# Softmax shift of both heads of a pair by VectorE, and rough maxima folded in SBUF, in a latent-attention and mixture-of-experts kernel

## The reference, cut to what matters

```python
x = x + layernorm(attention(layernorm(x)))      # x: (1, 2048, 256), float32
x = x + layernorm(moe(layernorm(x)))            # 16 experts of width 128, top 2, one shared expert

def attention(x):                               # 16 heads, latent keys and values of rank 64
    q = (x @ wq)                                # 128 + 64 columns a head, the 64 rotated
    ckv, k_pe = split(x @ wkv_a)                # 64 + 64, rms-normalised, rotated
    k_nope, v = split(ckv @ wkv_b)
    scores = einsum(q, k) * 192 ** -0.5         # causal mask
    attn = softmax(scores)
    return einsum(attn, v) @ wo
```

## Time and profile before

| | us |
|---|---|
| median of 3 runs | 1501.66 |
| lowest and highest of them | 1495.69, 1503.52 |
| span of the profiled execution, first to last instruction | 1484.4 |
| median of the runs less that span | 17.3 |
| TensorE matmul busy | 1299.4 (88%) |
| VectorE busy | 935.3 (63%) |
| GpSimd busy | 851.6 (57%) |
| ScalarE busy | 644.3 (43%) |

### The profile page before, as it was taken

How to read it: one execution, slowest core, us unless ns; L and a number is a source line. 1 busy time by engine, 2 the same in 40 slices (tenths; PEclk the granted TensorE clock), 3 DMA queues, 4 the chain that set the end, 5 groups by cost and what they waited for, 6 DMA issues and landing times.

```text
span 1484.4 us, 26542 instructions
## 1 busy us (share of the span) xinstructions
PE 1299.4 (88%) x7260; PEld 634.1 (43%) x7261; DVE 935.3 (63%) x2026; ACT 644.3 (43%) x1321; POOL 851.6 (57%) x900
## 2 busy tenths in 40 slices
PE   3989988899999789999999979999999999868830
PEld 2544564344446423333334632333333333647620
DVE  5555557654534777777663687767777683565536
ACT  3553535244443514444444432444444445347632
POOL 0073426566662747777777364778777778225535
PEclk9999999799999969999999977999999999979975
DMA  8000000000000000000000000000000000046754
GB/s 276 1 1 0 0 15 29 1 0 0 0 0 15 29 1 1 0 0 0 0 0 15 29 22 11 22 21 11 11 21 21 21 11 11 15 112 189 194 143 131
DMA packets 42931, 51.26 MB, mean 35 GB/s; under 512 B 5824, under 2 KB 39744, under 8 KB 42432
## 3 DMA queue, kind: packets, MB, share of 16 engines
q1 hardware_dynamic: 36816, 37.37, 8.1%
q0 software_dynamic: 4864, 10.51, 3.2%
...
## 4 chain that ended last, share of the span: by engine, by line
PE 69%; DVE 13%; issue 6%; POOL 5%; DMA 3%; ACT 3%; DVEq 0%; POOLq 0%; SPq 0%; ACTq 0%
PE ps L1386 17%; PE ps L1202 10%; PE ps L1333 9%; PE ps L1203 9%; PE ps L1204 9%; PE ps L1362 5%; DVE mxp L834 4%; PE ps L1478 2%; DMA B<-xn_rows,tok_i 2%; POOL C L404 1%; DMA B<-in_L_attn_x 1%; POOL A L411 1%; PE ps L1462 1%; POOL C L408 1%; PE ps L1364 1%
## 5 line engine op out<-in xcount | busy, mean ns | idle before, releaser
L395 POOL TENSOR_TENSOR D<-D,B 128x512 f32<-128x512 f32 (+3 forms) x512 | 551.6, 1094 | 118.4 <-ACT B L525 112.7
L525 ACT ACTIVATE B<-ps 128x512 f32<-128x512 f32 (+3 forms) x640 | 335.0, 533 | 530.5 <-DVE ps L854 209.5
L834 DVE TENSOR_REDUCE mxp<-ps 128x1 f32<-128x512 f32 (+3 forms) x640 | 378.5, 605 | 190.6 <-PE ps L1333 130.0
L1386 PE MATMUL ps<-B,kv 128*64 128x512 f32 (+3 forms) x1280 | 290.1, 549 | 0.0
L1333 PE MATMUL ps<-KTh,A 128*128 128x512 f16 (+3 forms) x640 | 233.5, 378 | 27.9 <-DVE mxp L834 18.5
L1202 PE MATMUL ps<-A,KTh 128*128 (+3 forms) x640 | 225.8, 353 | 2.7 <-issue 2.3
L1203 PE MATMUL ps<-A,KTh 128*128 (+3 forms) x640 | 224.6, 351 | 0.0
L1204 PE MATMUL ps<-A,KTl 128*128 (+3 forms) x640 | 223.9, 350 | 0.0
L854 DVE TENSOR_TENSOR ps<-ps,D 128x512 f32<-128x512 f32 x224 | 143.2, 639 | 92.2 <-PE ps L1364 54.9
L388 POOL TENSOR_TENSOR D<-B 128x512 f32<-128x512 f32 (+1 forms) x64 | 76.3, 1199 | 195.8 <-ACT B L525 195.8
L1333 PEld LDWEIGHTS ps<-KTh,A 128*128 (+1 forms) x640 | 62.9, 99 | 227.7 <-issue 118.6
...
...
## 6 DMA issues: line engine op xcount, KB each, us to landing
...
```

Source lines behind the costliest of these rows:

```text
L395: nc.gpsimd.tensor_tensor(acc[:, c0:], acc[:, c0:], Pr[:, i % P_RING, c0:], ALU.add).then_inc(sum_done, 1)
L525: nc.scalar.activation(Pr[:, i % P_RING, c0:], ps[:, i % ST_RING, c0:], ACT.Exp, scale=SM_SCALE).then_inc(exp_done, 1)
L834: V.tensor_reduce(mxp[:, s, i4, kc:kc + 1], ps[:, 4 + j % MX_RING, 0:w], AX.X, ALU.max).then_inc(mx_free, 1)
L1386: T.matmul(ps[LORA * s:LORA * (s + 1), BK_O, c0:], kv[:, kt, 0:LORA], Pr[:, i % P_RING, c0:], start=(kt == 0), stop=(kt == KT - 1)).then_i ...
```

## The change

The fourth matmul and `Dm` go, in all chunks. VectorE shifts both heads of a pair in all chunks, in one add over the two banks of a key tile (`shift`), and ScalarE takes exp over two banks in one instruction, GpSimd adds both heads in one. The scores ring is two pairs of banks (`ST_RING = 2`), the ring of probabilities four pairs (`P_RING = 4`); both hold as many key tiles as before.

The rough scores come in batches of two matmuls into the two banks 4 and 5 (`BK_X`; for a chunk's first pair also 0, 1 and 2, 3). ScalarE copies a batch to SBUF as bf16 (`take_rough`). VectorE folds there with `max` (`refine`): step by step the chunks of 512 keys into the first, then the half into the half down to 64 columns, then one reduction to `mrow`. TensorE spreads the maxima with four matmuls of `mrow` broadcast by a negated identity (`spread`), and ScalarE copies them out (`widen`). `early`, `refine_at` and `spread_at` say at which key tile of the pair each of these stands. The values of the last two key tiles of a pair move behind the first scores of the next pair, and the copy of the output with them.

```diff
-        CR_EXP, CR_PV, CR_SUM, CR_MX, CR_L, CR_O, CR = ST_RING, P_RING, P_RING, MX_RING, 2, 1, 2
+        CR_EXP, CR_PV, CR_SUM, CR_MX, CR_M, CR_L, CR_O, CR = ST_RING, P_RING, P_RING, 1, 2, 2, 1, 2
+        def batch(qc, b):
+            s, r = b // (tiles_of(qc) // 2), b % (tiles_of(qc) // 2)
+            kc, i0 = r // 2, 2 * (r % 2)
+            return s, kc, i0, CQ if kc < qc else P * (i0 + 2)
...
+        def early(qc):
+            n, every = tiles_of(qc), {0: (1, 2), 1: (2, 3), 2: (3, 4), 3: (3, 4)}[qc]
...
+                take = min(n - b, 2 if kt % every[0] == 0 else 1)
...
+        def spread_at(qc):
+            n = tiles_of(qc)
+            return (n - 3, n - 1) if qc > 1 else (n - 2, n - 1)
...
-                            nc.gpsimd.tensor_tensor(acc[:, c0:], acc[:, c0:], Pr[:, i % P_RING, c0:],
+                        nc.gpsimd.tensor_tensor(acc[:, :, c0:], acc[:, :, c0:], Pr[:, kt % P_RING, :, c0:],
...
+            def take_rough(qc, p, b):
+                act.wait_ge(mx_ready, first_kt(qc) + p * tiles_of(qc) + b + 1)
...
+                copy(dst[:, i0:i0 + 2, 0:w], ps[:, bk:bk + 2, 0:w]).then_inc(mx_out, 1)
+            def widen(qc, p, s):
+                act.wait_ge(wide_ready, 2 * (qc * NP + p) + s + 1)
+                copy(minus_m[:, p % 2, s, :], ps[:, BK_M, :]).then_inc(wide_done, 1)
+                for kt in range(KT):
+                    if len(new):
+                        take_rough(qc, p + 1, new[0])
+                    act.wait_ge(shifted, n + 1)
+                    nc.scalar.activation(Pr[:, kt % P_RING, :, c0:], ps[:, 2 * (kt % ST_RING):2 * (kt % ST_RING) + 2, c0:],
+                                         ACT.Exp, scale=SM_SCALE).then_inc(exp_done, 1)
+                    if kt == LAG - 1 and behind:
+                        values_out(qc, p - 1)
+                    if len(new) > 1:
+                        take_rough(qc, p + 1, new[1])
+                    if ahead and kt in spread_at(qc):
+                        widen(qc, p + 1, spread_at(qc).index(kt))
...
+            def refine(qc, p, s, k):
+                base, ring = rough(qc)
+                acc, chunk = base[:, s], ring[:, (s * qc + k) % 2]
+                if k:
+                    dve.wait_ge(mx_step, done)
...
+                if k == folds(qc) - 1:
+                    V.tensor_reduce(mrow[:, s, :], acc[:, :, 0:P // 2], AX.X, ALU.max).then_inc(m_ready, 1)
+                elif k >= max(qc, 1):
+                    h = (P // 2) << (folds(qc) - 2 - k)
+                    V.tensor_tensor(acc[:, :, 0:h], acc[:, :, 0:h], acc[:, :, h:2 * h], ALU.max).then_inc(mx_step, 1)
...
+                elif k == qc - 1:
+                    for i in range(TC):
+                        w = P * (i + 1)
+                        V.tensor_tensor(acc[:, i, 0:w], acc[:, i, 0:w], chunk[:, i, 0:w], ALU.max
+                                        ).then_inc(mx_step, 1)
+                else:
+                    V.tensor_tensor(acc, acc, chunk, ALU.max).then_inc(mx_step, 1)
             def shift(qc, p, kt):
-                V.tensor_tensor(ps[:, i % ST_RING, c0:], ps[:, i % ST_RING, c0:], minus_m[:, p % 2, c0:],
+                V.tensor_tensor(ps[:, bk:bk + 2, c0:], ps[:, bk:bk + 2, c0:], minus_m[:, p % 2, :, c0:],
                                 ALU.add).then_inc(shifted, 1)
+                for kt in range(KT):
+                    shift(qc, p, kt)
                     if ahead:
+                        for s, k in refine_at(qc)[kt]:
+                            refine(qc, p + 1, s, k)
+                    if kt == KT // 4 and sums is not None:
                         part_sums(qc, sums)
...
-                        ins = T.matmul(dst, ones4, Dm[:, p % 2, s, c0:], start=False, stop=(j < 0))
+                def spread(p, s):
+                    pe.wait_ge(m_ready, CR_M + k + 1)
+                    for j in range(TC):
+                        ins = T.matmul(ps[:, BK_M, j * P:(j + 1) * P], mrow[:, s, j:j + 1].broadcast_to([P, P]),
+                                       negident, start=True, stop=True)
+                    for kt in range(KT):
+                        new = early(qc)[kt] if ahead else ()
+                        scores(p, kt)
+                        if len(new):
+                            rough_batch(p + 1, new[0])
+                        if kt >= LAG:
+                            values(p, kt - LAG)
+                        elif behind:
+                            values(p - 1, KT - LAG + kt)
+                        if len(new) > 1:
+                            rough_batch(p + 1, new[1])
+                        if ahead and kt in spread_at(qc):
+                            spread(p + 1, spread_at(qc).index(kt))
```

More of the change, by code:

```diff
@@ new lines, in folds, with step_incs, folds_before, step_base @@
+        def folds(qc):
+            return qc + 4 if qc else 3
+        def step_incs(qc, k):
+            if qc == 0:
+                return (3, 1, 0)[k]
+            return ((1,) * (qc - 1) + (TC, 1, 1, 1, 0))[k]
+        def folds_before(qc, s, k):
+            return s * sum(step_incs(qc, i) for i in range(folds(qc))) + sum(step_incs(qc, i) for i in range(k))
+        def step_base(qc, p):
+            return sum(NP * folds_before(q, 2, 0) for q in range(qc)) + p * folds_before(qc, 2, 0)
+        def step_needs(qc, s, k):
+            last = s * (qc + 1) + (min(k + 1, qc) if qc else 0)
+            return 2 * last + 2
@@ new lines, in early, with refine_at @@
+        def early(qc):
+            n, every = tiles_of(qc), {0: (1, 2), 1: (2, 3), 2: (3, 4), 3: (3, 4)}[qc]
+            out, b = [], 0
+            for kt in range(n):
+                take = min(n - b, 2 if kt % every[0] == 0 else 1)
+                out.append(range(b, b + take))
+                b += take
+            return out
+        def spread_at(qc):
+            n = tiles_of(qc)
+            return (n - 3, n - 1) if qc > 1 else (n - 2, n - 1)
+        def refine_at(qc):
+            n, out, todo = tiles_of(qc), [], [(s, k) for s in range(2) for k in range(folds(qc))]
+            done = 0
+            for kt in range(n):
+                now = []
+                while todo and step_needs(qc, *todo[0]) <= done and (len(now) < 2 or kt == n - 1):
+                    now.append(todo.pop(0))
+                out.append(now)
+                done += len(early(qc)[kt])
+            return out
@@ L1339, in turn_max, with rough_batch @@
[L1339 to L1349 removed]
+                KT = tiles_of(qc)
+                def rough_batch(p, b):
+                    s, kc, i0, _ = batch(qc, b)
+                    n = first_kt(qc) + p * KT + b
+                    bk = rough_bank(p, b)
+                    pe.wait_ge(mx_out, n + 1 if bk == BK_X and b == 0 or not isinstance(p, int) or p
+                               else first_kt(qc) + max(b - 2, 0) + 1)
+                    for i in range(2):
+                        w = CQ if kc < qc else P * (i0 + i + 1)
+                        wide = w if qc else P * (i0 + 2)
+                        ins = T.matmul(ps[:, bk + i, 0:wide], QTh[:, bass.ds((2 * p + s) * CQ + (i0 + i) * P, P)],
+                                       KTh[:, kc * CQ:kc * CQ + wide], start=True, stop=(kc < qc))
+                        if kc == qc:
+                            ins = T.matmul(ps[:, bk + i, w - P:w], identb, mask_qk, start=False, stop=True)
+                    ins.then_inc(mx_ready, 1)
@@ L1377, in values @@
+                    for s in range(2):
+                        bk = 2 * (kt % ST_RING) + s
+                        q = bass.ds((2 * p + s) * CQ + c0, CQ - c0)
+                        ins = three(ps[:, bk, c0:], KTh[:, keys], KTl[:, keys], QTh[:, q], QTl[:, q], True, j < 0)
+                        if j >= 0:
+                            ins = T.matmul(ps[:, bk, c0:c0 + P], identb, mask_kq, start=False, stop=True)
+                    ins.then_inc(st_ready, 1)
                 def values(p, kt):
@@ L1407, in pair @@
+                    ins.then_inc(pv_done, 1)
+                def pair(p, ahead=True, behind=True):
                     for kt in range(KT):
-                        score_unit(p, 2 * kt)
-                        between()
-                        score_unit(p, 2 * kt + 1)
-                        between()
+                        new = early(qc)[kt] if ahead else ()
+                        scores(p, kt)
+                        if len(new):
+                            rough_batch(p + 1, new[0])
@@ L1421, in _ @@
                     pe.wait_ge(where_ready, qc)
-                for j in range(U):
-                    max_unit(0, j)
-                    if j == U // 2 + 2:
-                        turn_max(0, 0)
-                turn_max(0, 1)
-                if qc >= SHIFT_FROM:
-                    for h in range(2):
-                        spread(0, h)
-                with pe.Fori(0, NP - 1) as p:
-                    pair(p, True)
-                pair(NP - 1, False)
+                for b in range(KT):
```

(11 more changed lines are left out.)

302 lines of the change are left out of this document (118 added, 184 removed).

## The result

| | before | after |
|---|---|---|
| median, us | 1501.55 (4 runs, 1495.69 to 1503.52) | 1655.53 (4 runs, 1649.91 to 1660.71) |
| ratio, with its 95% interval | | 1.1044 (1.1001 to 1.1087) |
| span of the profiled execution | 1484.4 | 1658.8 |

The kernel became 10% slower: the direction of the forecast, but 111 us beyond its 1544 and 50 beyond the range. The span grew by 174.4 us, the median by 154. The profile of before lies 17 us under its median, that of after 3 over its own. A run's time is about 2 us above its own span (1660.71 and 1658.8 in the profiled execution of after), so the profiled execution of before was itself some 15 us faster than the median.

The account below looks back on a forecast made before the run. TensorE was taken to bound the pairs before; after, VectorE's work, waits and idle time. Pairs +56, last pairs -9 and first rough maxima -5 gave +42: span 1526 us, median 1544 us, range 1420 to 1605.

Parts of the forecast that it names:

- Folds by bytes: VectorE's bf16 folds: priced at half the fp32 row's time per element, 0.08 us + 0.52 ns per element.
- Rival D: VectorE's folds cost the fp32 row's price per element and bound the pairs: +120 us, 1664 us; chance 0.05.
- VectorE's work: Shifts, folds, part sums and cuts per pair: 30.3, 21.5, 14.4 and 7.3 us in chunks 3 to 0.
- its waits: VectorE's folds and cuts waiting for GpSimd's adds, per pair: 14.7, 9.2, 7.5, 2.5 us in chunks 3 to 0.
- period per pair = work + waits + idle: VectorE's time as the pair's period: 50.0, 35.7, 25.6 and 11.3 us in chunks 3 to 0.
- the pairs' term: Longer periods of seven pairs in each chunk: 7 x 8.05 = +56 us.
- rival C: Halfway: waits of three quarters of those forecast leave the pairs unchanged, 1495 to 1509 us; chance 0.07.
- Rival B: VectorE's waits fit into slack, under half of 14.7 us in chunk 3's pairs: faster, 1437 us; chance 0.33.
- Rival E: TensorE's stops at pair ends bring the low clock for a fifth of each pair: 1610 us; chance 0.05.
- Last pairs: Each chunk's last pair has no folds and only loses its row matmuls: -9 us.
- First rough maxima: Maxima for each chunk's first pair: chunk 3 from 25.9 to about 20.5 us, -5 us in all.
- Costed at nothing: Constants, semaphore setting and the moved output copy lie beside the next pair's matmuls: nothing, otherwise at most 1 us a chunk.

Follow-up runs that it names:

- after_no_adds: The changed kernel with GpSimd's adds cut to one column per head, except the first of each pair; 1492.64 us, ratio 0.996 to the kernel before.
- after_no_folds: The changed kernel with each VectorE fold cut to one column, GpSimd's adds whole; 1534.43 us, ratio 1.0258 to the kernel before.
- after_half_adds: The changed kernel with each GpSimd add split in two, one of 512 columns per head; 1617.93 us, ratio 1.0817 to the kernel before.
- after_heads: The changed kernel with scores, shift and exp done head by head instead of over two banks; 1644.92 us, ratio 1.099 to the kernel before.
- before_no_adds: The kernel before with GpSimd's adds one column wide except the first of each head and pair; 1497.56 us, ratio 0.9993 to the kernel before.

## Why the prediction was wrong

**The mechanism was right.** It was taken from two cuts that folds and adds shut each other out. after_no_adds and after_no_folds show from either side that both are needed for the loss, after_half_adds that a single fold waits by the length of an add. The Trainium skill (SBUF — State Buffer, Who interferes with whom) has it as a rule, and these runs agree, with 1.22 us alone and up to 3.34 beside an add.

**The prices were right.** Folds by bytes: 1.22 us for 2048 (1.2 taken), 0.35 for 384 (0.28), and 1.02 for the four small ones (1.0). Rival D is out. The shift is 1.14 from start to start, adds are 2.36 us in the median and 3.23 at the longest (2.37 and 3.5).

**VectorE's work was right, its waits right or too high.** Its busy time per pair in after_no_adds, where nothing waits, is 30.2, 21.5, 14.6 and 7.3 us in chunks 3 to 0, against 30.3, 21.5, 14.4 and 7.3. In after its busy share of the windows times the period gives 44.1, 28.8, 19.4 and 7.7. The differences are the waits: 13.9, 7.3, 4.8 and 0.4 us against 14.7, 9.2, 7.5 and 2.5. Chunk 3 came out nearly as counted, the shorter chunks had fewer waits. By kind in chunk 3, the single folds wait 4.1 us (4.5 taken), the runs 8.1 (6.6), the short groups nothing (1.0), the cuts 2.2 (2.6).

**The step that failed is the idle time in "period per pair = work + waits + idle".** I gave VectorE 5.0, 5.0, 3.7 and 1.5 us, "in a pair's first three key tiles". What is left of the period is 10.5, 12.2, 8.6 and 4.7. Over one pair of each chunk that is 20.8 us of idle too few against 7.4 of work and waits too many; the net 13.4, times seven, is 94, and the pairs' term missed by 149 - 56 = 93. Most of this idle time lies where I had put it, and is longer. Here are the first four shifts of a pair of chunk 3, in after and then in after_no_adds:

```profile
1226.13 1.23 DVE L959 TENSOR_TENSOR ps<-ps,D 128x1024 f32<-128x1024 f32 x1 [3.26 <-PE ps L1288]
1229.58 1.23 DVE L959 TENSOR_TENSOR ps<-ps,D 128x1024 f32<-128x1024 f32 x1 [2.21 <-PE ps L1288]
1231.81 1.23 DVE L959 TENSOR_TENSOR ps<-ps,D 128x1024 f32<-128x1024 f32 x1 [0.99 <-PE ps L1288]
1235.12 1.23 DVE L959 TENSOR_TENSOR ps<-ps,D 128x1024 f32<-128x1024 f32 x1 [2.08 <-PE ps L1288]
```

```profile
1044.81 1.23 DVE L959 TENSOR_TENSOR ps<-ps,D 128x1024 f32<-128x1024 f32 x1 [2.09 <-PE ps L1288]
1048.26 1.23 DVE L959 TENSOR_TENSOR ps<-ps,D 128x1024 f32<-128x1024 f32 x1 [2.21 <-PE ps L1288]
1050.49 1.23 DVE L959 TENSOR_TENSOR ps<-ps,D 128x1024 f32<-128x1024 f32 x1 [1.00 <-PE ps L1288]
1053.80 1.23 DVE L959 TENSOR_TENSOR ps<-ps,D 128x1024 f32<-128x1024 f32 x1 [2.08 <-PE ps L1288]
```

In after VectorE stands idle 8.5 us before these four, and 1.8 later in the pair. Without adds it is 7.4 before the same four, and the distances are the same to 0.01 us (3.45, 2.23, 3.31). So in these key tiles TensorE sets the pace, folds or not. Only before the first shift does after have 1.2 us more, where TensorE's first scores run at the low clock. The bare sum of matmuls, 40.9 us a pair, was too low a base for that pace: no kernel with both heads shifted came under 45.5, adds or not. My 2.8 us a key tile is a mean; from the first shift to the second it is 3.45 (1226.13 to 1229.58), with two rough batches, of which the second waits 0.71 us for ScalarE's copy of the one before (1227.65).

The second error is that I made the pair's period of one engine's time. Late in the pair VectorE sets the pace: from the shift at 1189.69 to the next it is 6.59 us, in after_no_adds 3.61 at the same place. Some of this is caught up within the pair, where the next three distances are 1.79, 2.05 and 4.39 us against 2.87, 2.84 and 3.53, but the first key tiles of the next pair give nothing back. The clock has 1.2 of chunk 3's 10.5 us, and the two-bank steps some 10 us of the kernel (after_heads). How the rest of the miss divides between the two errors no run separates.

**The range was narrower than its own working.** The waits of the sum are 33.9 us over the four chunks, times seven 237. A quarter less is 1485 us and a third more 1623, not 1510 and 1580, and rival C's three quarters give 1485, not 1495 to 1509. The measured waits were smaller than taken, so this is not what failed.

**Rival B** fell: the waits didn't fit into slack. It needed them gone, and with them gone (after_no_adds) the time was 1493, not 1437. **Rival E** named a thing that is there, at about a fifth of its price (13 us, as estimated above, of the 66 between 1610 and 1544).

**Last pairs.** -9 was forecast. A chunk's pairs less seven periods are 7.9, 21.4, 28.7 and 40.1 us before, and 11.8, 23.2, 31.0 and 39.7 after: +8. Row matmuls go there too, so something takes their gain and more; that the first and last key tiles of a chunk wait for VectorE is a guess. **First rough maxima.** -5 forecast, 6.2, 12.7, 20.0, 25.9 became 9.5, 14.0, 16.4, 19.1: -6. The rows of after that answer to the earlier trace rows:

```profile
984.88 1.03 PE L1421 MATMUL ps<-KTh,A 128*128 128x512 f16 x2 [1.42 <-issue]
...
1003.95 0.63 PE L1286 MATMUL ps<-A,KTh 128*128 128x512 f16 x1
```

**Costed at nothing.** Between chunks +6, and after the last values 232.9 us against 214.7. But that part is 224 to 233 in every other kernel here, 227.8 in before_no_adds, whose code there is that of before. So most of these 18 us looks like the scatter of one profiled execution, and it makes up most of the difference between the 174 us of the spans and the 154 of the medians.
